# A narrow-head attention stage rescheduled: transposed exponentials copied by ScalarE, expert rows added one pick a step, scores over 64 partitions, the output bias added by TensorE

## What is computed

```python
q = (_rms(x, g_q) @ Wq + bq)          # x is layer-normed; 16 heads of d = 16
kv = (_rms(x, g_kv) @ Wkv + bkv)      # k and v likewise
scores = einsum('bhqd,bhkd->bhqk', _rms(q, g_head), _rms(k, g_head)) * d ** (-0.5)
attn = softmax(scores, axis=-1)
out = (attn @ v).transpose(...).reshape(B, T, D) @ Wo + bo
x = x + out
```

## Time and profile before

| | |
|---|---|
| median of 3 runs | 1902.86 us (1897.18 to 1907.22) |
| the profiled execution | 1888.95 us, span 1887.1 us |
| busy, share of the span | PE 88%, DVE 66%, ACT 48%, POOL 30% |
| projections of the context | 1010.3 to 1083.3 us of the span |
| loop of steps, with its tail | 1083.3 to 1400.4 us of the span |

### The profile page before, as it was taken

How to read it: one execution, slowest core, us unless ns; L and a number is a source line. 1 busy time by engine, 2 the same in 40 slices (tenths; PEclk the granted TensorE clock), 3 DMA queues, 4 the chain that set the end, 5 groups by cost and what they waited for, 6 DMA issues and landing times. The chain is left out here.

```text
span 1887.1 us, 25728 instructions
## 1 busy us (share of the span) xinstructions
PE 1651.7 (88%) x8566; PEld 1317.9 (70%) x8566; DVE 1247.0 (66%) x2655; ACT 897.2 (48%) x2548; POOL 561.0 (30%) x447
## 2 busy tenths in 40 slices
PE   6999978978998786999999877789788999999866
PEld 5878867866877665767777655667567887788644
DVE  4654775787678757544444566766557778877878
ACT  4534533433443343323322245456446666666756
POOL 2133332643253054411002554646202122211000
PEclk9999998988999988999999967879689999999989
DMA  7143432622343143233434210100021111000001
GB/s 263 63 136 126 142 104 81 215 95 95 118 143 116 71 126 100 76 99 120 129 107 134 90 45 23 34 12 23 1 106 35 39 41 41 12 1 1 1 1 45
DMA packets 87511, 151.50 MB, mean 80 GB/s; under 512 B 9940, under 2 KB 45396, under 8 KB 87380
## 3 DMA queue, kind: packets, MB, share of 16 engines
q1 hardware_dynamic: 81236, 133.07, 21.6%
q0 software_dynamic: 6144, 16.79, 2.8%
HBM read 90.84 MB, written 58.98 MB: 79 GB/s over the span
## 5 line engine op out<-in xcount | busy, mean ns | idle before, releaser
L2330 ACT ACTIVATE self_attention<-self_attention,small 128x128 f32<-128x128 f32 x256 | 100.0, 392 | 122.4 <-DVE small L1647 122.4
L2489 ACT ACTIVATE narrow_late<-bank,small 128x128 f32<-128x128 f32 x256 | 90.7, 366 | 136.2 <-DVE small L1884 136.2
L783 PE MATMUL bank<-self_attention 128*128 128x256 f32 x512 | 133.7, 408 | 12.3 <-DVE residual L1666 12.3
L2567 ACT ACTIVATE cross_attention_heads<-cross_attention_heads,small 128x128 f32<-128x128 f32 x256 | 99.6, 390 | 89.2 <-DVE small L2021 89.2
L1115 PE MATMUL bank<-cross_attention,cross_attention_heads 128*128 128x256 f32 x512 | 124.7, 387 | 15.3 <-DVE residual L2035 10.1
L783 PEld LDWEIGHTS bank<-self_attention 128*128 128x128 f32 x512 | 103.4, 206 | 32.2 <-DVE residual L1666 15.4
L2671 POOL CAST qkv_weights_split<-self_attention 128x1024 fp32r<-128x1024 f32 x45 | 50.1, 1113 | 254.5 <-DMA self_attention<-in_wqkv 197.5
L587 PE MATMUL bank<-x_channel_major,qkv_weights_split 128*128 128x512 f32 x256 | 117.9, 461 | 8.6 <-ACT self_attention L2320 4.0
L1115 PEld LDWEIGHTS bank<-cross_attention,cross_attention_heads 128*128 128x128 f32 x512 | 95.5, 191 | 38.7 <-DVE residual L2035 19.0
L2673 POOL TENSOR_TENSOR qkv_weights_split<-self_attention,qkv_weights_split 128x1024 fp32r<-128x1024 f32 x45 | 107.2, 2382 | 3.6
L881 PE MATMUL bank<-experts,tiles 128*128 x316 | 107.6, 463 | 0.2 <-DVE tiles L1773 0.2
(11 more groups left out here) (384 smaller groups left out, 4805.6 us busy)
## 6 DMA issues: line engine op xcount, KB each, us to landing
picked_inputs<-self_attention SPq DMA_DIRECT2D x64, 512.0 KB, 6.6
self_attention<-in_wqkv SPq DMA_DIRECT2D x48, 512.0 KB, 6.3
experts_far<-picked_inputs SPq DMA_DIRECT2D x79, 128.0 KB, 2.1
picked_outputs<-tiles SPq DMA_DIRECT2D x79, 128.0 KB, 1.7
self_attention<-in_wo SPq DMA_DIRECT2D x16, 512.0 KB, 4.1
experts<-in_moe SPq DMA_DIRECT2D x4, 1408.0 KB, 13.7
self_attention<-in_bv SPq DMA_DIRECT2D x16, 256.0 KB, 5.2
context_values<-context_out SPq DMA_DIRECT2D x16, 256.0 KB, 2.2
```

Source lines behind the costliest of these rows:

```text
L783: m = T.matmul(bank[7][:, 0:D], ZT_a[n % 2][:, h, :], wo_a[p % 2][:, h, :], start=h == 0, stop=h == HG - 1)
L2330: m = S.activation(P_a[u][:, h, :], P_a[u][:, h, :], ACT.Exp, bias=negmax_a[u][:, h:h + 1], accum_out=sums_a[u][:, h:h + 1])
L2489: m = S.activation(n_P[v][:, h, :], s4_in[:, h, :], ACT.Exp, bias=n_negmax[v][:, h:h + 1], accum_out=n_sums[bb % 2][:, q4 * 4 + h:q4 * 4 + ...
L2567: m = S.activation(P_x[u][:, h, :], P_x[u][:, h, :], ACT.Exp, bias=negmax_x[u][:, h:h + 1], accum_out=sums_x[u][:, h:h + 1])
```

## The change

It does the following:

1. The copies of the transposed exponentials move from DVE to ACT, where the copy for n - 2 stands before `exps(n)`; on PE the transposes stand before the scores of the step.
2. `combine` is cut into single picks, one a step on DVE (COMBINE: batch 8 + n // 4), with the gathers one pick a step on GpSimd (GATHER) and a fourth row buffer. Batches 0 to 7 are combined before the loop (0 to 3 before).
3. Scores use 64 partitions: four heads in each half, and the spread keys have half the columns (`mask4`).
4. The output bias is added by two further matmuls of `narrow_output`, identity times the bias in two parts; `narrow_bias` is gone.
5. The squares of the cross keys move ahead of the loop, as four ACT squares a batch that also sum, into bank 7; `sum_keys` is gone; the inverse is one instead of two; KEY_NORM and KEY_TURN become 32 + c and 50 + c.
6. Moments and norm of a group are done in halves over two steps each. Projections are taken out a step later, head norms likewise, and the four projections of group 0 come after all keys and values. Two instead of four `narrow_heads` stand before the loop.
7. In the self-attention stage the PE's turn of w_y comes two pieces later.

```diff
-NXS, NYS, NYG = 4, 3, 3
+NXS, NYS, NYG = 4, 3, 4
+FIRST_STEPS = [(g, 16 * (g - 1)) for g in range(1, NG)]
+MOMENTS = {n + half: (g, half) for g, n in FIRST_STEPS for half in range(2)}
+NORMALISE = {n + 2 + half: (g, half) for g, n in FIRST_STEPS for half in range(2)}
+CHANNELS = {n + 4: g for g, n in FIRST_STEPS}
+PROJECT = {n + 6 + b: GB * g + b for g, n in FIRST_STEPS for b in range(GB)}
+ROOT = {n + 11: g for g, n in FIRST_STEPS}
+HEADS = {1: 2, 2: 3, **{n + 13 + b: GB * g + b for g, n in FIRST_STEPS for b in range(GB)}}
+GATHER = {n: (9 + n // TOPK, n % TOPK) for n in range((B - 9) * TOPK)}
+COMBINE = {n: (8 + n // TOPK, n % TOPK) for n in range((B - 8) * TOPK)}
...
@@ wkv_chunk (PE)
-                yield from pause(15)
+                yield from pause(17)
                 pe.wait_ge(wkv_y, c + 1)
...
-                yield from pause(2)
@@ narrow_scores (PE)
-                T.matmul(bank[2 + n % 2][:, :], n_qT[bb % 8][:, q4 // 2, :],
-                         kbd[bb % 2][:, q4 // 2, (q4 % 2) * 4:(q4 % 2) * 4 + 4, :].rearrange("p h t -> p (h t)"),
+                i, half = divmod(q4, 2)
+                rows = slice(half * P // 2, (half + 1) * P // 2)
+                T.matmul(bank[2 + n % 2][:, :], n_qT[bb % 8][rows, i, :], kbd[bb % 2][rows, i].rearrange("p h t -> p (h t)"),
@@ narrow_output (PE)
+                for part in range(2):
+                    T.matmul(bank[7][:, 256:512], ident_r, (n_bo_hi, n_bo_lo)[part], start=part == 0, stop=False)
                 for i in range(2):
-                    m = T.matmul(bank[7][:, 256:512], n_zT[bb % 2][:, i, :], n_wo[:, i, :], start=i == 0, stop=i == 1)
+                    m = T.matmul(bank[7][:, 256:512], n_zT[bb % 2][:, i, :], n_wo[:, i, :], start=False, stop=i == 1)
@@ combine (DVE)
+            def combine_pick(bb, k):
+                g, c = bb // GB, bb * TOPK + k
                 dve.wait_ge(gathered[bb % NYG], 16 * TOPK * (bb // NYG + 1))
                 settle_x(g)
+                V.scalar_tensor_tensor(out=X[:, bb, :], in0=y_rows[bb % NYG][:, k * D:(k + 1) * D], scalar=pick_weight[:, c:c + 1],
+                                       in1=X[:, bb, :], op0=ALU.mult, op1=ALU.add).then_inc(combined, 1)
@@ square_keys (ACT)
+                for h in range(NKV):
+                    c = bb * NKV + h
+                    m = S.activation(bank[7][:, h * P:(h + 1) * P], x_key[bb][:, h * P:(h + 1) * P], ACT.Square,
+                                     accum_out=kss[:, c:c + 1])
@@ the copy, from the DVE program to the ACT program
-                V.tensor_copy(n_PT[n % 2], four(bank[4 + n % 2][:, :])).then_inc(n_PTs, 1)
+                S.copy(n_PT[n % 2], four(bank[4 + n % 2][:, :])).then_inc(n_PTs, 1)
@@ spread_keys (POOL)
-                    m = G.tensor_tensor(kbd[s][:, i], n_kT[bb % 8][:, i].unsqueeze(1).broadcast_to([P, 8, P]),
-                                        mask8.unsqueeze(2).broadcast_to([P, 8, P]), ALU.mult)
+                    m = G.tensor_tensor(kbd[s][:, i], n_kT[bb % 8][:, i].unsqueeze(1).broadcast_to([P, HG, P]),
+                                        mask4.unsqueeze(2).broadcast_to([P, HG, P]), ALU.mult)
```

More of the change, by code:

```diff
@@ L383, in build @@
         late_qT = [ar.take(2 * P) for _ in range(2)]
-        kbd = [ar.take(2 * 8 * P).rearrange("p (i h t) -> p i h t", i=2, h=8) for _ in range(2)]
-        ar.take(512)
+        kbd = [ar.take(2 * HG * P).rearrange("p (i h t) -> p i h t", i=2, h=HG) for _ in range(2)]
+        late = ar.at
+        wr = columns(scope, "narrow_bias_split", P + 2 * D, F32R)
+        ident_r, n_bo_hi, n_bo_lo = wr.take(P), wr.take(D), wr.take(D)
+        ar = columns(scope, "narrow_later", 2 * NSH * (UW + DW) - late - wr.width)
+        y_rows = [ar.take(TOPK * D)]
+        ar.at = ar.width - 2 * 2 * P
         late_qT += [ar.take(2 * P) for _ in range(2)]
@@ L397, in build @@
         qss = ar.take(2 * GB * 32).rearrange("p (s b c) -> p s b c", s=2, b=GB)
-        y_rows = [ar.take(TOPK * D) for _ in range(NYG)]
-        mask8 = sm.take(8)
+        y_rows += [ar.take(TOPK * D) for _ in range(NYG - 1)]
+        mask8, mask4 = sm.take(8), sm.take(HG)
         gg = sm.take(2)
@@ L968, in narrow_channels @@
             def narrow_channels(g, kt):
+                to, filled, read, use = xt_use(NORM["second", g], kt)
                 pe.wait_ge(n_heads, GB * (g - 1) + 3 + kt)
-                turn_xt(NORM["second", g], kt)
+                pe.wait_ge(read, use - kt)
+                turn_norm(NORM["second", g], kt, to).then_inc(filled, 1)
             def narrow_scores(n):
@@ L1951, in vector_program @@
+            narrow_sums(GB - 1)
+            combine(5)
+            narrow_inverse(0)
+            combine(6)
+            combine(7)
+            for n in range(B * 4 + 6):
+                if n >= 7 and (n - 7) % 4 == 0 and n < B * 4 + 4:
+                    narrow_values((n - 7) // 4)
                 if n < B * 4:
                     narrow_scores(n)
-                    if g + 1 < NG:
-                        when = NEXT_GROUP[g + 1]
-                        if u in when["combine"]:
-                            combine(GB * (g + 1) + when["combine"].index(u))
-                        if u == when["moments"]:
-                            moments(NORM["second", g + 1])
-                        if u == when["norm"]:
-                            normalised(NORM["second", g + 1])
-                        if u == when["channels"]:
-                            split_xt(NORM["second", g + 1], 0)
-                            split_xt(NORM["second", g + 1], 1)
-                        if u in when["project"]:
-                            narrow_project(GB * (g + 1) + when["project"].index(u))
-                        if u == when["bias"]:
-                            narrow_bias(g + 1)
-                        if u == when["inverse"]:
-                            narrow_inverse(g + 1)
-                        if u in when["after"]:
-                            combine(GB * (g + 2) + when["after"].index(u))
@@ L1990, in take_queries @@
+                if n in CROSS_MOMENTS:
+                    moments(NORM["cross", CROSS_MOMENTS[n]])
+                if n in CROSS_NORM:
+                    normalised(NORM["cross", CROSS_NORM[n]])
+                if n in CROSS_SPLIT:
+                    split_xt(NORM["cross", CROSS_SPLIT[n][0]], CROSS_SPLIT[n][1])
+                if n >= 9 and (n - 9) % 4 == 0:
+                    narrow_output((n - 9) // 4)
             def take_queries(f):
```

364 lines of the change are left out of this document (183 added, 181 removed).

## The result

The changed kernel takes 1955.6 us (median of four runs, 1938.6 to 1985.5) against 1902.2 us for the kernel before: a ratio of 1.025, 95% interval 1.015 to 1.035. (The ratio is that of the fast executions; the one of 1985.5 us counts as a slow one and is left out of it.) It is slower, where 1848 us was forecast. Its profiled execution took 1944.5 us, 55.6 us more than that of before, which took 1888.95. I split the difference at TensorE's landmarks, the experts' last tile, the first score and the last output product.

A forecast was written before the change was run, and what follows sets the result against it. The loop was taken to lose by PE's waits, chiefly for DVE, and by half-speed work. Loop 45, ahead of it 0 and w_y turn 10 made 55 us: 1834 us profiled, 1848 against the median; 8-in-10 range 1815 to 1886.

The forecast's parts named there:

- A score streams 512 columns before and after, so PE gains nothing: Loop's scores over 64 partitions: no change in PE time, nothing put in the sum.
- a score holds PE longer than before at full clock: Loop's scores: a sign named in advance that would show the prediction wrong; no size given.
- The rival of the drain: Loop's scores: emptying the array costs 0.16 us twice a step, 20 us in all, giving 1868 us; chance 0.15.
- The loop's gain: Loop with its tail: 317.1 us falls to about 269, taken as 45 us gained, bounds 20 and 85.
- Bank-0 waits: Loop steps with projections: PE waits about 1.9 us for DVE to free bank 0, three times per 16 steps, 5.7 us.
- The start of the loop: First pick of batch 8 on DVE waits for its rows, so steps 1 to 4 come some 7 us late.
- Ahead of the loop: Between last projection and first score: 9 us of idle PE, net change 0, from -3 to +6 us.
- The w_y turn: Self-attention stage: turning w_y two pieces later gains 10 us, bounds 0 and 16.
- ScalarE as the bound: Loop: copies waiting for transposes hold the next exponentials, 0.6 us a step, 38 of 45 us gone, 1886 us; chance 0.10.
- Its 57 us in the last 16 steps: Loop steps 48 to 63: ACT's busy time rises from 47.3 to 57 us, as a sign over 80% busy.
- Gathers at the head of DVE's queue: Loop: DVE stops every fourth step for a batch's fetches, 7 to 10 us a batch, up to 1918 us; chance 0.06.
- GpSimd beside DVE: Loop: shorter GpSimd spreads, 0.96 instead of 1.91 us, hold DVE's norms and picks less; left out of the sum.

The follow-up runs named there:

- best_64: best with the scores over 64 partitions, by turns lower and upper half, spreads of keys as for 128: 1904.6 us, ratio 1.015 to the kernel before.
- best: start with scores ahead of transposes and DVE taking a projection out of bank 0 ahead of the step's maximum: 1834.3 us, ratio 0.977 to the kernel before.
- filler: The kernel after with one useless matmul over all 128 partitions ahead of each score: 1898.4 us, ratio 1.012 to the kernel before.
- full_filler: full_rows with one useless matmul over all 128 partitions ahead of each score: 1878.3 us, ratio 1.000 to the kernel before.
- before_again: The kernel before, unchanged, for a second profile: 1880.0 us, ratio 1.001.
- start: full_rows with GpSimd's gather of block 7 moved from ahead of the first head norm to behind the first spread of keys: 1853.1 us, ratio 0.987.
- wy_alone: The kernel before with only the turn of w_y two pieces later: 1892.2 us, ratio 0.995.
- full_rows: The kernel after with scores over all 128 partitions again, all else of the change kept: 1879.1 us, ratio 0.986 to the kernel before.
- full_rows_2: full_rows unchanged, as a later reference and second profile: 1853.2 us, ratio 0.986 to the kernel before.
- after_again: The kernel after, unchanged, for a second profile: 1970.0 us, ratio 1.036 to the kernel before.
- half_rows_alone: The kernel before with only the scores taken over 64 partitions, every order and copy kept: 1951.7 us, ratio 1.025.

## Why the prediction was wrong

- **"A score streams 512 columns before and after, so PE gains nothing"** is the step that failed. (Of the signs that I named, it was "a score holds PE longer than before at full clock" that showed.) The term was put at nothing, and it cost 70 us (best_64 against best). Some 20 us of that are the changes of the row count, 0.29 to 0.35 us a score (filler against full_filler); the other 50 or so, a difference and not a measurement, go with the clock.
- *The rival of the drain* had the mechanism and the size of its own part: 0.16 us a change and 20 us forecast, 0.17 and 19 to 22 us measured. What neither it nor any other case had was that such passes also take the clock away. I had reckoned with stretches at half speed as a thing that comes of idle time, and the earlier trace rows suggested that, since the clock was low where the waits were. The kernel after has fewer waits and a lower clock.
- *The loop's gain* was mis-sized too. Without the 64 rows it is 18 to 20 us on one chip (before_again's 314.0 to start's 295.7, wy_alone's 314.5 to full_rows' 294.5), at the lower bound that I gave and not 45. I had reckoned it as waits that go. But idle time in the loop hardly fell, from 57 us to 51 and 56 in full_rows and full_rows_2, and TensorE's work became shorter with half-clock time down from 131 us to 69 and 62. Bank-0 waits (14.8 us in nine, 1.6 each) came as forecast; what I hadn't in the sum are waits for DVE's z, 16.5 us in full_rows_2, and the order of scores.
- *The start of the loop* was right. The timeline of DVE in the kernel after shows the first pick of batch 8 (7 us forecast):

```profile
1099.23 2.97 DVE L1758 SCALAR_TENSOR_TENSOR residual<-narrow_later,dispatch,residual 128x256 f32<-128x256 f32 x1 [6.15 <-DMA narrow_later<-picked_outputs,dispatch]
```

- *Ahead of the loop* the idle time was 11.0 us (9 forecast), and on a chip without unexplained stops the stretch grew by 4.3 us, inside -3 to +6; the profiled pair's 16.7 is outside. *The w_y turn* was right in size by the times (10 us in wy_alone) and by the last tile on the second chip, 7 to 8 us earlier. On the first chip it doesn't show in that landmark: 1015.7 and 1017.4 us in full_rows and after_again, which have it, 1016.6 in half_rows_alone, which doesn't.
- *ScalarE as the bound* didn't come: its copies waited for TensorE. Its 57 us in the last 16 steps did come, but of 92 us, which is 62% and not over 80. *Gathers at the head of DVE's queue* cost once, at the start.
- *GpSimd beside DVE.* The norm of 5.78 us in the earlier trace rows has one tensor input, and GpSimd wasn't scaling keys then: the trace has a spread (L2820) and the split of the query weights (L2833, L2835). The picks, with two inputs in SBUF, bear out what the prediction says of such operations: about 0.48 us each behind the experts without elementwise work of GpSimd beside them, 1.9 us on average with it in full_rows, 1.3 in after with its shorter spreads. DVE's busy time in the loop is 142.7 us in full_filler and 127.5 in filler, but DVE wasn't what the loop waited for.
- Had the scores stayed on 128 rows, 1879 us would have been measured against 1904, a gain of 25 us where 55 was forecast. On the second chip, start against before_again: 8 us before the experts' last tile, -2 to the first score, 18 in the loop, 3 behind it.

Left open: why the clock answers to passes over 64 rows and hardly to 96, and whether it is the rows or the gap at each change of them. The runs show that it does, not how the chip counts. Open is also why the price in the order of before (half_rows_alone) ran from 12 to 50 us. filler tried one amount of work over all rows beside them; how little of it is enough wasn't tried.

## What to carry to other kernels

A matmul over 64 partitions took no less time here than one over 128, held TensorE 0.3 us longer among matmuls over 128, and left the stage's clock at 0.67 where it was 0.89. Fill the rows, with zeros if need be. When TensorE is busy all the time and its clock column stays low, look at the shapes of its passes before its waits, and compare its busy time per instruction with the profile before: a rescheduling that removes waits shows nothing if each instruction got longer. And idle time that falls may only be covered by slower work: the kernel after had less of it than the faster full_rows.

## What was unexpected of the hardware

- Useless work made a kernel faster: 128 passes of 512 columns over all rows brought the loop from 365 to 373 us down to 335, with the clock from 0.68 to 0.91.
- TensorE was busy 98.8 of 102.4 us at 1.2 GHz without a rise.
- 96 rows kept a clock of 0.87 where 64 rows in the same steps had 0.80 and 128 had 0.89.
- The weights of a 64-row matmul behind one over 128 rows weren't loaded under it, and neither were those of the next one over 128: 0.3 to 0.35 us a round at full clock.
- TensorE stood 7.0 and 7.4 us for nothing that the profile shows, in the context's projections of some executions, with the kernel before's code there as well.
